# An attention and feed-forward block: one group of value products per kv head, rotated rows and late pages on GpSimd, new rank shifts

## The chip, the cores and the metric

One core of a Trainium2 chip runs the whole program. Time is device time in microseconds (us) from start to end of one execution. The core's engines are TensorE (PE; its weight loads are PEld), VectorE (DVE), ScalarE (ACT), GpSimd (POOL) and SyncE (SP), which here issues most of the DMAs. Each has a queue of its own that runs in program order; between queues there are semaphores.

## What is computed

```python
q = (x @ wq).reshape(4, 512, 32, 32); k, v = (x @ wk), (x @ wv)   # 8 kv heads of 32
q, k = _apply_rope(q, cos, sin), _apply_rope(k, cos, sin)
k, v = jnp.repeat(k, 4, axis=2), jnp.repeat(v, 4, axis=2)
scores = einsum('bqhd,bkhd->bhqk', q, k) / sqrt(32) + causal_mask
out = einsum('bhqk,bkhd->bqhd', softmax(scores), v).reshape(4, 512, 1024) @ wo
x = _layernorm(x + out)
gate_w, up_w, down_w = gate_t * gate_s[:, None], up_t * up_s[:, None], down_t * down_s[:, None]
x = _layernorm(x + (silu(x @ gate_w.T) * (x @ up_w.T)) @ down_w.T)   # 1024 -> 3584 -> 1024
```

x is 4 x 512 x 1024 in float32; gate_t, up_t and down_t are integers from -1 to 1.

## The kernel before

A float32 operand is held as two float16 parts, an upper one (a copy rounded to float16) and a lower one (what is left), and a product of two such operands is three matmuls. Work goes in 128-row tiles: 4 batches of 4 tiles. Attention is done in 16 units of 8 query heads, which is 2 kv heads each, and the code names a kv head of a unit by G. In order:

- **Pages.** Slices of x, wq, wkv and wo arrive by DMA as pages of 128x1024 (`page_load` on SP), ScalarE makes the upper part (`split_hi`, L1241) and VectorE the lower part (`split_lo`, L1384). The first 12 pages (`NFIRST`) have room of their own; the 24 late ones (wq of the units 2 and 3, all of wo, x of the batches 1 to 3) go through two buffers in turn, so a load waits for both parts of the page two before.
- **Projections** (L1070) into two banks by turns. For q and k VectorE forms two products with the rope tables (`rotate`, L1403 and L1405), GpSimd adds them (`rope_add`, L1631), ScalarE writes the upper part twice into rows to be stacked (`nat_hi`, L1257: 128x256 in, read twice, 128x512 out), GpSimd the lower part (`nat_lo`, L1638), and a DMA transposes the rows into q_stack or k_stack (`stack` on SP, L1703). There are 80 such rows: 64 of q, 16 of k. Two buffers (`NNAT`) are used in turn.
- **Row sums.** `score_q` (L1086) makes the scores with queries on the rows, VectorE takes the maximum (`row_max`, L1414 to L1420), ScalarE the sum of the exponentials (`row_sum`, L1280), and maxima and logarithms of the sums become three more rows of q_stack (`max_rows`, by DMA).
- **Products with the values.** `score_k` (L1111) makes the scores with keys on the rows, so that the exponential (`exp`, L1266) gives the final weights in p_tiles. For each kv head the key tiles go from 3 down to 0, with 128, 256, 384 and 512 query columns for each of 4 heads, in 1, 2, 4 and 4 instructions. GpSimd zeroes the upper triangle of the diagonal block (`causal`, L1645). TensorE multiplies with the values (`pv`, L1127) in float32, 4 heads side by side in the array, in groups of `VALUE_TILES` = 2 key tiles: tiles 3 and 2 as one group, which starts when tile 2 is masked, tiles 1 and 0 as another, which starts when tile 0 is masked. Every tile has one buffer in p_tiles. ScalarE and VectorE copy the bank out in two parts (`att_hi`, L1273, `att_lo`, L1457).
- **Output projection** (also L1070), layer norm (`norm_stats` on VectorE, `newton` on GpSimd, L1652 to L1656, `norm` on ScalarE), and seven forms of the result per pair of tiles (`x1_form` on GpSimd, `x1_hi`, `x1_lo`), stored and loaded again transposed as x_forms (L1760).
- **Feed-forward part**, from about 680 us on: seven products instead of eight for gate and up (L1170) and for most of down (L1211), the last ones plain (L1195).

The order in every queue is fixed when the kernel is built. `Plan.put` (L269) gives each piece an engine, a rank in us, an assumed duration, and the pieces that it follows; to the rank the number for its kind in `SHIFTS` (L232) is added. `Plan.close` (L279) then walks through time and gives every engine, whenever it is free, the able piece with the smallest rank. Pairs of kinds in `AT_ONCE` (L246) may follow each other on one engine with no assumed delay. The result is only an order; the semaphores decide when a piece runs.

## Time and profile before

| | us |
|---|---|
| median of 3 runs (1777.97 to 1781.43) | 1781.22 |
| the profiled execution | 1779.99 |
| its span, first to last instruction | 1778.2 |
| busy: TensorE | 1711.6 |
| busy: VectorE | 1208.3 |
| busy: ScalarE | 967.4 |
| busy: GpSimd | 409.1 |

The profile is one execution. Busy time counts an instruction from start to end; a matmul's end is modelled, and matmuls overlap, so a busy TensorE may still lose a little between them. Lines are those of the kernel's source. A wait is put down to the engine that released it last. The granted clock of TensorE is given as a share of full speed; 1.00 is 2.4 GHz.

### The profile page before, as it was taken

Reading aid. Unit: us, or ns where it says so; the run is one execution under the profiler, and the core shown is the slowest. Engines: PE = TensorE matmul, PEld = TensorE weight load, DVE = VectorE, ACT = ScalarE, POOL = GpSimd, SP = SyncE. Lnnn points to the kernel's source line nnn. Section 1 sums busy time; section 2 is a strip of 40 time slices with the busy share of each in tenths; the row PEclk is TensorE's granted clock in tenths of the full one; section 3 lists DMA queues with packets and bytes.
Section 4 is the critical chain, followed back from the end, with each engine's and each line's share of the span. In section 5 each row is a group of like instructions: output and inputs, shape, how many; then the busy total and the mean of one; then the engine's idle time right before and its main releaser. Section 6 shows DMA issues by size and latency. Waiting matters only on the chain.

```text
span 1778.2 us, 26642 instructions
## 1 busy us (share of the span) xinstructions
PE 1711.6 (96%) x9456; PEld 824.8 (46%) x9456; DVE 1208.3 (68%) x2593; ACT 967.4 (54%) x2201; POOL 409.1 (23%) x782
## 2 busy tenths in 40 slices
PE   7979999999999999999999999999999999999998
PEld 4634555555455434444444444444444444443444
DVE  7776668478667744677877768746667666678456
ACT  6799989789978874472553543531323233231321
POOL 3324445445434442410000002103100000003113
PEclk9999999999999999999999999999999999999999
DMA  8543345335235698582653545658312112133202
GB/s 266 104 141 61 70 114 144 61 96 155 56 67 138 163 222 297 170 300 95 207 173 130 202 159 194 219 146 195 115 60 87 42 65 86 42 110 106 96 13 83
DMA packets 228004, 233.44 MB, mean 131 GB/s; under 512 B 183200, under 2 KB 183840, under 8 KB 227872
## 3 DMA queue, kind: packets, MB, share of 16 engines
q1 hardware_dynamic: 224704, 222.86, 42.9%
q10 hardware_dynamic: 3168, 8.88, 1.3%
q8 instruction: 75, 1.23, 0.3%
q14 instruction: 57, 0.47, 0.1%
HBM read 122.78 MB, written 72.88 MB: 110 GB/s over the span
## 4 chain that ended last, share of the span: by engine, by line
PE 71%; DVE 9%; DMA 8%; ACT 8%; issue 2%; POOL 1%; SPq 1%; DVEq 0%; ACTq 0%; POOLq 0%
PE bank L1170 31%; PE bank L1070 13%; PE bank L1211 12%; PE bank L1195 6%; ACT bank L1280 3%; PE bank L1111 3%; PE bank L1127 3%; PE bank L1086 2%; DMA w_page<-gateT 2%; DMA x_forms<-x_forms_spill 1%; ACT p_tiles L1266 1%; DMA w_page<-upT 1%; DMA q_stack<-max_rows 1%; DMA x_forms_spill<-x_parts 1%; DVE acc L1620 1%
## 5 line engine op out<-in xcount | busy, mean ns | idle before, releaser
L1170 PE MATMUL bank<-x_forms,weight_forms 128*128 128x512 f16 x3136 | 705.0, 379 | 7.8 <-DVE up_blocks L1566 4.1
L1170 PEld LDWEIGHTS bank<-x_forms,weight_forms 128*128 128x128 f16 x3136 | 305.4, 98 | 382.4 <-issue 9.9
L1280 ACT ACTIVATE bank<-bank,row_max 128x512 f32<-128x512 f32 (+3 forms) x512 | 265.3, 541 | 21.1 <-DVE row_max L1420 13.5
L1211 PE MATMUL bank<-down_forms 128*128 128x512 f16 x1120 | 267.4, 379 | 7.3 <-DVE acc L1601 7.3
L1420 DVE CUSTOM_DVE_ANT_0 bank<-bank,cmask 128x256 f32<-128x256 f32 (+2 forms) x384 | 206.6, 580 | 85.4 <-PE bank L1086 84.3
L1266 ACT ACTIVATE p_tiles<-bank 128x512 f32<-128x512 f32 (+1 forms) x352 | 194.7, 597 | 44.2 <-PE bank L1111 42.8
L1070 PE MATMUL bank<-wq_parts,xT_parts 128*128 128x256 f16 x1536 | 204.3, 276 | 8.6 <-DVE wq_parts L1380 8.0
L1601 DVE TENSOR_TENSOR acc<-bank,acc 128x512 f32<-128x512 f32 x248 | 167.2, 686 | 59.3 <-PE bank L1211 58.0
L1662 POOL TENSOR_TENSOR acc<-acc,down_forms 128x1024 f32<-128x1024 f32 x16 | 40.2, 2527 | 695.6 <-DVE acc L1601 695.6
L1645 POOL TENSOR_SCALAR_AFFINE_SELECT p_tiles<-p_tiles 128x128 f32<-128x128 f32 (+2 forms) x352 | 123.7, 358 | 231.2 <-ACT p_tiles L1266 227.9
L1211 PEld LDWEIGHTS bank<-down_forms 128*128 128x128 f16 x1120 | 108.7, 98 | 142.2 <-DVE acc L1601 13.1
L1070 PEld LDWEIGHTS bank<-wq_parts,xT_parts 128*128 128x128 f16 x1536 | 150.6, 99 | 49.8 <-DVE wq_parts L1380 8.0
L1070 PE MATMUL bank<-wo_parts,att_parts 128*128 128x512 f16 x672 | 163.6, 380 | 3.3 <-DMA att_parts<-att_spill 3.2
L1086 PE MATMUL bank<-k_stack,q_stack 96*128 96x512 f16 (+3 forms) x512 | 118.8, 302 | 16.9 <-ACT bank L1280 9.4
L1111 PE MATMUL bank<-q_stack,k_stack 99*128 99x512 f16 (+1 forms) x352 | 117.6, 365 | 12.5 <-DMA q_stack<-max_rows 6.0
L1360 ACT ACTIVATE down_forms<-gate_blocks 128x512 f16<-128x512 f32 x92 | 57.6, 626 | 131.6 <-DVE gate_blocks L1576 120.9
L1280 ACT ACTIVATION_READ_ACCUMULATOR bank<-bank,row_max 128x1 f32 x512 | 126.3, 247 | 0.0
L1566 DVE TENSOR_TENSOR up_blocks<-bank,up_blocks 128x512 f32<-128x512 f32 x84 | 57.8, 689 | 96.8 <-ACT up_blocks L1337 67.3
L1348 ACT ACTIVATE gate_blocks<-gate_blocks,gate_scale 128x512 f32<-128x512 f32 x84 | 60.3, 719 | 106.4 <-DVE gate_blocks L1566 106.4
L1195 PE MATMUL bank<-down_forms 128*128 128x512 f16 (+1 forms) x528 | 110.9, 373 | 0.0
L1070 PEld LDWEIGHTS bank<-wo_parts,att_parts 128*128 128x128 f16 x672 | 64.8, 98 | 75.2 <-issue 6.6
L1337 ACT ACTIVATE up_blocks<-bank 128x512 f32<-128x512 f32 x84 | 49.9, 594 | 88.9 <-PE bank L1170 88.7
(124 smaller groups left out, 1990.8 us busy)
## 6 DMA issues: line engine op xcount, KB each, us to landing
weight_forms_spill<-weight_forms SPq DMA_DIRECT2D x28, 896.0 KB, 5.6
weight_forms<-weight_forms_spill SPq DMA_DIRECT2D x28, 896.0 KB, 4.6
...
```

The costliest lines, as they stand in the source:

```text
L1070: t = nc.tensor.matmul(dst, left[:, a, k, rows], right[:, c, k, cols], start=k == 0 and m == 0, stop=last)
L1086: t = nc.tensor.matmul(to[:, h, :], qT[0:STK, u % QS, h0 + h, i * P:n], kT[0:STK, b % 2, kv_of(u, h0 + h), 0:n], start=h == 0, stop=h == R ...
L1111: nc.tensor.matmul(to, kT[0:STKM, b % 2, (u % UNITS) * UG + G, lo:lo + P], qT[0:STKM, u % QS, heads, lo:S], start=True, stop=True).then_in ...
L1170: t = nc.tensor.matmul(strassen[bank_set(use)][to][:, :], w_form[:, use % 4, A_FORMS[a_form], k * P:(k + 1) * P], xF[:, :, B_FORMS[b_form] ...
L1195: t = nc.tensor.matmul(to[:, 0:cols.stop - cols.start], hid_p[place_of(r)][:, k, a, i // 2 * P:(i // 2 + 1) * P], wd_p[place_of(r)][:, c, ...
L1211: t = nc.tensor.matmul(to[:, :], hid_f[r % NF % 3][:, HID_FORMS.index(a_form), a, pair * P:(pair + 1) * P], wd_f[r % NF % 3][:, DOWN_B[b_f ...
L1266: nc.scalar.activation(p32[j][:, h0:h0 + heads, :], bank[5 + m % 2][:, 0:heads * n].rearrange("p (h c) -> p h c", c=n), ACT.Exp, scale=SCO ...
L1280: nc.scalar.activation(scores, scores, ACT.Exp, scale=SCORE_DOWN if mask_added(i) else -1.0, bias=mx[:, u % 2, i, h:h + 1], accum_out=row_ ...
L1348: nc.scalar.activation(gate_t[:, k, :], src, ACT.Silu, scale=sg[:, 2 * (n % NF) + r:2 * (n % NF) + r + 1]).then_inc(s_silu, 1)
L1420: t = nc.vector.tensor_tensor_reduce(scores[:, h, :], scores[:, h, :], cmask[:, S - n:S], -SCORE_DOWN, -MASKED, ALU.add, ALU.min, mx[:, u ...
L1601: nc.vector.tensor_tensor(dst, got[:, :], dst, ALU.add).then_inc(s_acc, 1)
L1645: nc.gpsimd.affine_select(out=block, in_=block, compare_op=ALU.is_ge, fill=0.0, base=0, pattern=[[0, KEY_HEADS[j]], [1, P]], channel_multi ...
```

## The change

Three things are changed together.

1. `VALUE_TILES` goes from 2 to 4: the products with the values of all four key tiles of a kv head are one group. It is issued when the last tile (0) is masked. Inside the group the order 3, 2, 1, 0 stays, and so do the counts that the next head's exponentials wait for.
2. `nat_hi` moves from ScalarE to GpSimd, as a tensor_copy with the same input and output, so that rope_add, nat_hi and nat_lo of a row all run on GpSimd. `split_hi` of the 24 late pages moves from ScalarE to GpSimd too, as a tensor_scalar multiplication, and counts on a semaphore of its own. A late page_load waits for the lower part alone. Two small DMAs that ScalarE issued ahead of a late page now go with the last first page.
3. All of `SHIFTS` is new, which changes the order in every queue, and two pairs are added to `AT_ONCE`.

The diff, its core:

```diff
@@ -90,7 +90,7 @@
 
 KEY_HEADS = (1, 1, 2, 4)
 
-VALUE_TILES = 2
+VALUE_TILES = 4
 KEY_USES = [(G, j, h) for G in range(UG) for j in reversed(range(NT)) for h in range(0, REP, KEY_HEADS[j])]
 NKEY = len(KEY_USES)
 
...
@@ -230,21 +230,21 @@
 
 
 SHIFTS = {
-    PE: {"down": 20, "max_tr": 17, "product": 45, "proj_out": -9, "proj_q": 126, "pv": 12, "score_k": 5, "score_q": 13},
-    SC: {"exp": 328, "hid_hi": -4, "ln_exp": 32, "nat_hi": 381, "norm": 21, "row_sum": 156, "silu": 43, "split_hi": 54,
-         "v_copy": -17, "w_cast": 233, "x1_hi": 8, "x1_store": 1},
-    VE: {"acc": 3, "add_x1": -55, "att_lo": 195, "bound": 21, "d_form": 40, "ds_scale": 6, "hid_form": 9, "hid_lo": 37,
-         "hidden": 55, "ln_seed": -2, "ln_step": 43, "max_copy": 218, "max_parts": 9, "norm_stats": 76, "residual": -4,
-         "rotate": -64, "row_max": 53, "split_lo": 31, "sum": 14, "w_form": 60, "x1_lo": 18},
-    PO: {"nat_lo": 7, "newton": -12, "rope_add": -45, "scale_row": 11, "x1_form": -2},
-    SY: {"att_load": -3, "att_store": 58, "bound_load": -34, "bound_store": -16, "d_in": -20, "d_store": 64, "ds_load": -20,
-         "last_x1": -2, "max_rows": -14, "out_store": 11, "page_load": -4, "row_load": -4, "stack": 11, "w_in": -30, "w_load": 19,
-         "w_store": -24, "xF_load": 130, "xF_store": 3},
+    PE: {"down": -1, "max_tr": 21, "product": 8, "proj_out": -4, "proj_q": 13, "pv": 23, "score_k": 9, "score_q": 17},
+    SC: {"att_hi": -8, "copy": -9, "exp": 29, "hid_hi": -1, "ln_exp": 3, "norm": -10, "row_sum": 35, "silu": 4, "v_copy": -118,
+         "w_cast": 64, "x1_hi": -171, "x1_store": 5},
+    VE: {"acc": -72, "add_x1": -45, "att_lo": 136, "bound": 6, "d_form": 3, "hid_form": -7, "hid_lo": 11, "hidden": 42,
+         "ln_seed": 33, "ln_step": 21, "max_copy": -9, "max_parts": 4, "norm_stats": 17, "residual": 122, "rotate": -2,
+         "row_max": 37, "split_lo": 93, "sum": -73, "w_form": 92, "x1_lo": -6},
+    PO: {"causal": 49, "nat_hi": -4, "nat_lo": -15, "newton": 56, "rope_add": 29, "scale_row": -9, "split_hi": 17, "x1_form": 59},
+    SY: {"att_load": 1, "att_store": -1, "bound_load": -29, "bound_store": -12, "d_in": 4, "d_store": 201, "ds_load": -33,
+         "last_x1": -45, "max_rows": -2, "out_store": 59, "page_load": -18, "stack": 4, "w_in": -18, "w_load": 10, "w_store": -16,
+         "xF_load": 72, "xF_store": -33},
 }
 
 
 AT_ONCE = {("sum", "hidden"), ("hidden", "hid_form"), ("hid_form", "hid_form"), ("ln_step", "max_parts"), ("d_form", "d_form"), 
-           ("residual", "norm_stats"), ("acc", "norm_stats"), ("x1_form", "x1_form"), ("ln_seed", "ln_step"), ("norm", "x1_store")}
+           ("residual", "norm_stats"), ("acc", "norm_stats"), ("x1_form", "x1_form"), ("ln_seed", "ln_step"), ("norm", "x1_store"), ("rope_add", "nat_hi"), ("nat_hi", "nat_lo")}
 
 
 class Waits:
...
@@ -357,7 +357,7 @@
         last = [loads[n - 1]] if n else []
         put(SY, at, .4, "page_load", what, b, j, moves=2 * FIRST_MOVES if n == 0 else FIRST_MOVES if n < NFIRST else PAGE_MOVES,
             after=[("split_lo", *loads[before])] if before >= 0 else [])
-        put(SC, at, .95, "split_hi", what, b, j, after=[("page_load", what, b, j)] + [("split_hi", *w) for w in last] + (
+        put(SC if n < NFIRST else PO, at, .95 if n < NFIRST else 1.4, "split_hi", what, b, j, after=[("page_load", what, b, j)] + [("split_hi", *w) for w in last] + (
             [("proj", "q", UNITS * b - 1, j, KD - 1)] if what == "x" and b else []))
         put(VE, at, 1.14, "split_lo", what, b, j, after=[("split_hi", what, b, j)] + [("split_lo", *w) for w in last])
 
...
@@ -417,7 +417,7 @@
         put(VE, -195.0 + 2 * t if one[0] == "q" and w == 0 and t < 2 else end, .72, "rotate", *one, after=[made] + ([("rotate", *one_back)] if r else []) + (
             [("nat_lo", *two_back), ("rope_add", *two_back)] if r > 1 else []))
         put(PO, end + 1, .68, "rope_add", *one, after=[("rotate", *one)])
-        put(SC, end + 2, .53, "nat_hi", *one, after=[("rope_add", *one)] + ([("nat_hi", *one_back)] if r else []) + ([("stack", *two_back)] if r > 1 else []))
+        put(PO, end + 2, .72, "nat_hi", *one, after=[("rope_add", *one)] + ([("nat_hi", *one_back)] if r else []) + ([("stack", *two_back)] if r > 1 else []))
         put(PO, end + 3, .68, "nat_lo", *one, after=[("nat_hi", *one)] + ([("nat_lo", *one_back)] if r else []))
         old = w - QS if one[0] == "q" else UNITS * (w - 1) - 1
         put(SY, end + 4, 1.25, "stack", *one, moves=TURN_MOVES, after=[("nat_lo", *one)] + ([("stack", *one_back)] if r else []) + (
...
@@ -1223,15 +1223,11 @@
                         e.dma_start(idH[:, :], identH).then_inc(s_const, 16)
                         e.dma_start(idB[:, :], identB).then_inc(s_const, 16)
                         e.dma_start(cmask[:, :], causal).then_inc(s_const, 16)
-                    elif n == NFIRST + 2:
+                    elif n == NFIRST - 1:
                         e.dma_start(sg[:, :], gate_s).then_inc(s_scale, 16)
                         e.dma_start(su[:, :], up_s).then_inc(s_scale, 16)
                     src, arrived, times = page_of(n)
                     on.wait_ge(arrived, 16 * times)
-                    if which[0] == "wo":
-                        on.wait_ge(s_lo, NFIRST)
-                    if which[0] == "x" and which[1]:
-                        on.wait_ge(s_proj, proj_n["q", which[1] * UNITS - 1, which[2]] + 1)
                     up = X_UP if which[0] == "x" else W_UP
                     hi, whole = parts_of(*which)[0], as_parts(which[0], src)
                     if n < HALVED:
...
@@ -1246,16 +1242,6 @@
                     on.wait_ge(s_pv, (b - 1) * UNITS * UG * NT)
                     nc.scalar.activation(v32[:, b % 2, t, :], bank[n % 2][:, nk:2 * nk], ACT.Copy,
                                          scale=PROJ_DOWN).then_inc(s_v, 1)
-                elif kind == "nat_hi":
-                    r = rot_n[which]
-                    on.wait_ge(s_add, r + 1)
-                    on.wait_ge(s_set, 1)
-                    on.wait_ge(s_stack[r % NNAT], 16 * (r // NNAT))
-                    rows = nat[:, r % NNAT, :, 0:STK].rearrange("p h (f c) -> p h f c", f=3)
-                    fields = slice(0, 3, 2) if which[0] == "k" else slice(0, 2)
-                    ta = ropeA[:, r % NNAT, :].rearrange("p (h c) -> p h c", h=UH)
-                    nc.scalar.activation(rows[:, :, fields, :], ta.unsqueeze(2).broadcast_to([P, UH, 2, HD]),
-                                         ACT.Copy).then_inc(s_nhi, 1)
                 elif kind == "exp":
                     u, G, j, h0 = which
                     m, q, heads, n = key_n(*which), u * UG + G, KEY_HEADS[j], S - j * P
...
@@ -1380,7 +1366,10 @@
                         nc.vector.scalar_tensor_tensor(lo[:, 0:mid], whole[:, 0:mid], up, hi[:, 0:mid],
                                                        ALU.mult, ALU.subtract).then_inc(s_half_lo, 1)
                         hi, lo, whole = hi[:, mid:], lo[:, mid:], whole[:, mid:]
-                    on.wait_ge(s_hi, n + 1)
+                    if n < NFIRST:
+                        on.wait_ge(s_hi, n + 1)
+                    else:
+                        on.wait_ge(s_hi_late, n - NFIRST + 1)
                     nc.vector.scalar_tensor_tensor(lo, whole, up, hi, ALU.mult, ALU.subtract).then_inc(s_lo, 1)
                 elif kind == "rotate":
                     what, w, t = which
...
@@ -1629,6 +1618,25 @@
                     on.wait_ge(s_proj_taken, taken["rotate", what, w, t])
                     to = ropeA[:, r % NNAT, :]
                     nc.gpsimd.tensor_tensor(to, to, ropeB[:, r % 2, :], ALU.add).then_inc(s_add, 1)
+                elif kind == "nat_hi":
+                    r = rot_n[which]
+                    on.wait_ge(s_add, r + 1)
+                    on.wait_ge(s_set, 1)
+                    on.wait_ge(s_stack[r % NNAT], 16 * (r // NNAT))
+                    rows = nat[:, r % NNAT, :, 0:STK].rearrange("p h (f c) -> p h f c", f=3)
+                    fields = slice(0, 3, 2) if which[0] == "k" else slice(0, 2)
+                    ta = ropeA[:, r % NNAT, :].rearrange("p (h c) -> p h c", h=UH)
+                    nc.gpsimd.tensor_copy(rows[:, :, fields, :], ta.unsqueeze(2).broadcast_to([P, UH, 2, HD])).then_inc(s_nhi, 1)
+                elif kind == "split_hi":
+                    n = split_n[which]
+                    src, arrived, times = page_of(n)
+                    on.wait_ge(arrived, 16 * times)
+                    if which[0] == "wo":
+                        on.wait_ge(s_lo, NFIRST)
+                    if which[0] == "x":
+                        on.wait_ge(s_proj, proj_n["q", which[1] * UNITS - 1, which[2]] + 1)
+                    nc.gpsimd.tensor_scalar(parts_of(*which)[0], as_parts(which[0], src), X_UP if which[0] == "x" else W_UP, None,
+                                            ALU.mult).then_inc(s_hi_late, 1)
                 elif kind == "nat_lo":
                     r = rot_n[which]
                     on.wait_ge(s_add, r + 1)
...
@@ -1687,7 +1695,6 @@
                     n = split_n[which]
                     dst, arrived, times = page_of(n)
                     if n >= NFIRST + 2:
-                        on.wait_ge(s_hi, n - 1)
                         on.wait_ge(s_lo, n - 1)
                     e.dma_start(as_parts(which[0], dst), source_of(*which)).then_inc(arrived, 16)
                 elif kind == "stack":
```

## Rows read from the trace of the kernel before

**Rows 1.** The page, busy time by engine: us, share of the span, instructions.

```profile
PE 1711.6 (96%) x9456; PEld 824.8 (46%) x9456; DVE 1208.3 (68%) x2593; ACT 967.4 (54%) x2201; POOL 409.1 (23%) x782
```

**Rows 2.** Stretches: busy us of PE, PEld, DVE, ACT, POOL; clock, DMA share, GB/s.

```profile
46.00:92.00 46.00, 41.68 (x342) 31.26 (x341) 36.70 (x119) 35.46 (x110) 17.65 (x27) 0.96 0.51 103
92.00:138.00 46.00, 35.45 (x235) 16.48 (x233) 34.76 (x103) 44.37 (x131) 13.88 (x34) 0.93 0.50 140
138.00:598.00 460.00, 450.52 (x3276) 243.12 (x3275) 313.89 (x971) 403.75 (x1185) 212.88 (x455) 1.00 0.40 96
598.00:690.00 92.00, 82.19 (x468) 32.73 (x465) 50.73 (x128) 63.23 (x151) 39.04 (x90) 0.98 0.96 232
690.00:1196.00 506.00, 496.99 (x2290) 222.46 (x2290) 361.10 (x608) 230.16 (x328) 51.14 (x47) 1.00 0.55 188
...
1250.00:1778.00 528.00, 515.47 (x2398) 233.69 (x2396) 341.90 (x545) 152.47 (x236) 40.65 (x66) 1.00 0.21 75
```

**Rows 3.** Waits in 46 to 138: who <- for whom, total us, times, longest.

```profile
PE bank L1086 <- ACT bank L1280: 5.8, 6, 2.6
...
PE bank L1111 <- ACT p_tiles L1266: 2.4, 4, 0.9
```

**Rows 4.** Waits in 138 to 598, same columns.

```profile
PEld bank L1111 <- ACT p_tiles L1266: 21.8, 57, 0.9
...
POOL stack_rows L1638 <- ACT stack_rows L1257: 16.1, 31, 2.8
PEld bank L1086 <- ACT bank L1280: 15.6, 46, 0.8
...
PEld bank L1127 <- POOL p_tiles L1645: 4.8, 14, 0.4
```

**Rows 5.** Waits of TensorE in 598 to 690.

```profile
PE bank L1070 <- DMA att_parts<-att_spill: 2.3, 2, 2.1
```

**Rows 6.** Timeline: start us, us, engine, line, instructions, [idle before <- releaser].

```profile
332.86 0.86 PE L1127 MATMUL bank<-p_tiles,v 128*32 128x128 f32 x16
...
333.65 0.39 PE L1111 MATMUL bank<-q_stack,k_stack 99*128 99x512 f16 x1
...
340.47 0.29 POOL L1645 TENSOR_SCALAR_AFFINE_SELECT p_tiles<-p_tiles 128x128 f32<-128x128 f32 x1 [0.19 <-ACT p_tiles L1266]
...
340.71 1.18 ACT L1266 ACTIVATE p_tiles<-bank 128x512 f32<-128x512 f32 x2
...
341.18 1.71 PE L1127 MATMUL bank<-p_tiles,v 128*32 128x384 f32 x16
...
342.82 0.55 PE L1111 MATMUL bank<-q_stack,k_stack 99*128 99x512 f16 x2
343.02 0.60 ACT L1273 ACTIVATE att_made<-bank 128x512 f16<-128x512 f32 x1 [0.61 <-PE bank L1127]
```

**Rows 7.** Groups of ScalarE in 92 to 138: count | busy us, mean ns | idle before.

```profile
L1241 ACT ACTIVATE wo_parts<-page 128x1024 f16<-128x1024 f32 x4 | 4.3, 1075 | 0.5 <-DMA page<-wo 0.5
L1257 ACT ACTIVATE stack_rows<-rope_cos 128x512 f16<-128x512 f32 x4 | 2.9, 734 | 0.0
L1241 ACT ACTIVATE xT_parts<-page 128x1024 f16<-128x1024 f32 x2 | 2.1, 1064 | 0.1
```

**Rows 8.** Groups of ScalarE in 138 to 598.

```profile
L1257 ACT ACTIVATE stack_rows<-rope_cos 128x512 f16<-128x512 f32 x58 | 38.9, 696 | 2.3 <-POOL rope_cos L1631 1.7 <-DMA q_stack<-stack_rows 0.5
...
L1241 ACT ACTIVATE xT_parts<-page 128x1024 f16<-128x1024 f32 x8 | 8.5, 1064 | 0.0
```

**Rows 9.** Groups of GpSimd by form, whole run.

```profile
L1662 POOL TENSOR_TENSOR acc<-acc,down_forms 128x1024 f32<-128x1024 f32 x16 | 40.2, 2527 | 695.6 <-DVE acc L1601 695.6
...
L1645 POOL TENSOR_SCALAR_AFFINE_SELECT p_tiles<-p_tiles 128x512 f32<-128x512 f32 x32 | 20.4, 639 | 31.2 <-ACT p_tiles L1266 31.2
...
L1672 POOL TENSOR_TENSOR x_difference<-row 128x512 f32<-128x512 f32 x7 | 8.9, 1274 | 8.1 <-ACT row L1299 8.1
```

**Rows 10.** One line's instructions: count, duration ns min/median/max, first and last start.

```profile
L1384 DVE SCALAR_TENSOR_TENSOR wq_parts<-page,wq_parts x4: 1224/1456/1749, 24.9 to 34.4; 128x1024 f16<-128x1024 f32 x4
```

8 lines of the change are left out of this document (4 added, 4 removed).

## Prediction

> **What bounds the kernel now.** Three runs gave a median of 1781.2 us. The profiled execution took 1780.0, of which 1778.2 is its span, so the sum below starts from 1780.0 and the median lies 1.2 above it. The first view to read is the page: TensorE is busy for 1711.6 us, 96% of the span, while ScalarE, VectorE and GpSimd have 54, 68 and 23% [rows 1]. So the kernel is bound by TensorE where its queue is full, and only two things can make it shorter: a matmul stream that needs less time, or idle TensorE time that is filled. The second view, the stretches, says where that idle time is [rows 2]. The reader takes TensorE's busy time from the length of each: 4.3 us of 46 are idle in 46 to 92, 10.6 in 92 to 138, 9.5 in the 460 us from 138 to 598, 9.8 in 598 to 690, 9.0 in 690 to 1196, and 12.5 in 1250 to 1778. In all that is 56 us (3.1%), which is about the ceiling of any better order; of the whole span 1778.2 - 1711.6 = 66.6 are idle, and the rest of that lies before 46.
>
> Which engine ends those waits differs by stretch. In 92 to 138 ScalarE is busy 44.4 of 46 us and TensorE's granted clock falls to 0.93. There, and in the stretch ahead of it, TensorE's waits name ScalarE: 5.8 us for row sums and 2.4 for exponentials, 8.2 of the 14.9 that are idle [rows 3]. In 138 to 598 ScalarE is at 403.8 of 460 (88%), and TensorE's weight loads wait for it 21.8 + 15.6 us [rows 4], most of which a running matmul covers, since TensorE is idle for 9.5 in all. In 598 to 690 the DMA share is 0.96, and a DMA, of att_parts, heads TensorE's waits [rows 2, 5]. After 690 the change moves no work between engines; ScalarE is busy less than half of that time.
>
> **One group of products instead of two.** A group of 16 records for the tiles 3 and 2 streams 128 + 256 = 384 columns; from its start to the next matmul's it takes 333.65 - 332.86 = 0.79 us. The group for the tiles 1 and 0 streams 512 + 384 = 896 columns in 342.82 - 341.18 = 1.64 [rows 6]. Taken as a fixed part plus a part per column, 0.85 us for 512 more columns is 1.66 ns a column, and 0.79 - 384 x 0.00166 leaves 0.15 us fixed. The 32 pairs of groups (16 units, 2 kv heads each) become 32 groups: 32 x 0.15 = 4.9 us of TensorE's time go. If the fixed part is an effect of the pipeline that next to no issue hides, all of it is gained; if it is drain that other waits swallow, nothing is. I take **-4.9**, bounds 0 and -5.
>
> **What the group now waits for.** It starts after the causal mask on the last exponentials (tile 0), and the exponentials of the next head may write tile 3 only when this group's product with tile 3 is done. Rows 6 show the present overlap. The last causal mask of one head begins at 340.47; ScalarE has the next head's first exponentials on at 340.71, before the second group starts at 341.18. With one group, started in the same place, tile 3 is free at 341.18 + 0.15 + 128 x 0.00166 = 341.54, and with the 0.2 us from an end to the engine it releases (the group ends at 342.82, ScalarE's copy of it starts at 343.02) ScalarE has it at about 341.75: the exponentials pause **1.0 us more per head**, 32 us in all. Queued behind them on ScalarE, in the order fixed when the kernel is built, stand row sums and later exponentials; behind the group on TensorE stand projections. Cover: for each kv head there are 16 row sums (one for each of 4 tiles of 4 heads), which can be placed in the pause, and TensorE has the projections' matmuls. If the cover is gone, each of the 32 costs up to 1.0 us. It is thinnest for the last kv heads, when all row sums are done. I take **+2**, bounds 0 and +32.
>
> **ScalarE is relieved.** 80 copies of rotated rows (0.70 us each) and 24 conversions of late pages (1.06) leave it [rows 8], 56 + 25 = 81 us. Where it is worth something: in 92 to 138 there are 4 copies and 6 conversions, 2.9 + 4.3 + 2.1 = 9.3 us [rows 7] of a full ScalarE, against 10.6 us of idle TensorE and a clock of 0.93 (46 x 0.07 = 3.2 us lost while busy or idle). I take 6 of the 9.3, since a wait on VectorE's maxima or a page's DMA may come close behind, and 1 for the clock: **-7**, bounds -12 and 0. In 138 to 598, 58 copies and 8 conversions, 38.9 + 8.5 = 47.4 us [rows 8], leave an engine that would then be at (403.8 - 47.4) / 460 = 77%; of the 9.5 idle us there I take **-2**, bounds -9 and 0.
>
> **GpSimd takes it.** The trace has neither operation there. The nearest row with one input is the mask of 128x512, 0.64 us (the same rows); with two inputs, 128x512 takes 1.27 and 128x1024 takes 2.53 [rows 9]. So a copy of 128x512 costs 0.64 to 1.27 and a conversion of 128x1024 1.28 to 2.53; both have one input, and I take the lower ends with a little more, 0.7 and 1.4: 80 x 0.7 + 24 x 1.4 = 90 us, at the upper ends 162. GpSimd is busy for 17.7 + 13.9 + 212.9 + 39.0 = 283 of the 644 us from 46 to 690 [rows 2], 44%; it becomes 58 to 69%. In the rotation's chain it saves two changes of engine (GpSimd stands 16.1 us waiting for ScalarE's copies in 138 to 598, rows 4), and the projections run a unit and more ahead of the scores that use them, so the chain itself costs nothing; without that lead, it is 80 x 0.2 us at most. What counts is what waits behind these on GpSimd: the causal masks, and behind the last of each head the products. 24 conversions of 1.4 us and 80 copies of 0.7 cover 90 of 640 us, so 14% of the 32 masks that release a group meet one, for half its length: 32 x 0.14 x 0.5 = 2.2 us. A page is also converted 0.4 us later and reloaded later; the loads lose a wait on the upper part that the wait on the lower part implies. I take **+1**, bounds 0 and +6. SP's queue keeps its instructions; it waits for other producers only.
>
> One thing could make these operations dearer. The same lower-part instruction on VectorE takes from 1.224 to 1.749 us [rows 10], so something in this kernel holds VectorE up. With each of the 24 late lower parts put off by 1.749 - 1.224 = 0.525, 12.6 us come onto VectorE, which is busy for 385 of the 552 us from 46 to 598 [rows 2]; that costs nothing in the sum, and at worst, if GpSimd's masks are held up in turn, the bound of +6. The Trainium skill (SBUF — State Buffer, section on the two physically separate sides) names a cause that speaks against the move: the port pair of these two engines is an exclusive lock, taken for a whole instruction by a GpSimd operation or by a VectorE operation with two SBUF inputs. The spread in rows 10 agrees with it; by that rule the sum would be the same or go to +6 here.
>
> **The new shifts** reorder every queue. q projections fall from 126 to 13, so they no longer only fill gaps; ScalarE's exponentials go from 328 to 29. No row prices that. In 598 to 690 there are 9.8 idle us to win; a reordering of x_forms loads and projections can win or lose 5. After 690 there are 21.5, of which the chain behind the last matmul stays. I take -1 for 598 to 690, **0** after, and keep 6 each way.
>
> **Sum.** -4.9 + 2 - 7 - 2 + 1 - 1 = -11.9; 1780.0 - 11.9 = 1768.1, and 1.2 for the median: **1769 us**, 0.7% faster. Its own range is 1762 to 1776.
>
> **The rivals.** *The relief does not arrive.* Another wait (VectorE's maxima, page DMAs) ends last in 92 to 138, and TensorE gets the 4.9 us less 3 of new waits: 1781.2 - 1.9 = 1779. For it: only in 92 to 138 is ScalarE full; in the 46 us before it stands idle for 10.5 itself, and the work of TensorE there does not shrink. Chance 0.15. *Slower: the ring of one group.* Exponentials, mask, products and next exponentials become one chain per head, 1.0 us longer, on engines whose order is fixed. The place is 138 to 690, where TensorE is 97% busy. It decides from the point where 14 of the 32 pauses reach TensorE, for the gains are 4.9 + 7 + 2 + 1 = 14.9 and GpSimd takes 1 of them. If three in four do, and the masks are 3 us late in all, it is 24 + 3 - 14.9 = +12: 1781.2 + 12 = 1793. Against it: now only 4.8 us of weight loads in 460 wait for a mask [rows 4]. Chance 0.24. *Slower by order alone:* the shifts cost 5 at 598 to 690 and 6 in the feed-forward part, nothing is gained but the groups: 1781.2 - 4.9 + 11 = 1787. Chance 0.06. *More is won:* the first stretches and the x_forms stage both close (-12 there, -5, -5 after 690, -5 for groups, +3): 1757. Chance 0.13. That the moved work shows no shorter ScalarE at all is excluded by the diff.
>
> **How the numbers follow.** The forecast has the remaining 0.42. Measurements of this kernel can tell about 0.2%, 3.6 us, from no change. Faster by more: 0.42 + 0.13 + 0.05 of the first rival = 0.60; within: 0.12, the rest of the first rival and what of the slower cases ends near; slower: 0.28. The range reaches from 1756 to 1790: it holds the forecast, the first rival, the order case, most of the larger gain and the nearer half of the ring.
>
> **What would show it.** Right: in the changed profile ScalarE falls by some 80 us and GpSimd rises by some 90; the products of a head stand as one run of 32 records of about 2.3 us; the idle time of TensorE near 92 to 138 is under 5 us with the clock near 1.00. Wrong: in 138 to 598 the weight loads' waits for exponentials, row sums and masks, now 21.8 + 15.6 + 4.8 = 42.2 us [rows 4], double; page conversions of over 2 us on GpSimd; or new idle time after 690, which would be the shifts'.

## The result and the profile after

The changed kernel is slower: 1798.3 us median of 4 runs (1794.09 to 1803.54) against 1781.3 of the kernel before (1777.97 to 1782.24, 4 runs). The ratio is 1.0085, with a 95% interval of 1.0059 to 1.0112. The forecast was 1769, and the time lies outside its range of 1756 to 1790. The profiled execution took 1794.09, and its span is 1792.4, 14.2 longer than before. Four executions of the runs further down were over 10% above their kernel's others, and the medians leave them out.

First the page of the changed kernel, busy time by engine (us, share of the span, instructions):

```profile
PE 1714.0 (96%) x9456; PEld 829.1 (46%) x9456; DVE 1220.8 (68%) x2593; ACT 906.0 (51%) x2097; POOL 530.8 (30%) x886
```

Against [rows 1], ScalarE lost 61 us (80 were expected) and GpSimd gained 122 (90 were expected). The group rows of the copies and conversions that left ScalarE add up to 53.2 + 25.5 = 78.7 us; the records of its instructions overlap in part, and the busy time counts an overlap once, so it fell by less. TensorE's idle time, span less busy time, went from 66.6 to 78.4 us, and its busy time rose by 2.4, though the products with the values went from 84.0 to 78.8. The 11.8 us of idle time and the 2.4 of busy time make up the 14.2.

The stretches of the changed kernel say where (busy us of PE, PEld, DVE, ACT, POOL; clock, DMA share, GB/s):

```profile
20.00:46.00 26.00, 21.44 (x123) 11.86 (x122) 16.72 (x20) 3.35 (x13) 25.62 (x16) 0.93 0.56 135
...
46.00:92.00 46.00, 41.17 (x316) 30.04 (x315) 38.44 (x133) 32.08 (x117) 35.96 (x44) 0.96 0.60 114
92.00:138.00 46.00, 38.25 (x295) 20.39 (x294) 33.73 (x88) 33.85 (x104) 45.85 (x51) 0.96 0.44 116
138.00:598.00 460.00, 433.35 (x3080) 233.69 (x3078) 316.89 (x953) 352.97 (x1086) 259.54 (x493) 0.98 0.41 97
598.00:690.00 92.00, 83.65 (x543) 36.84 (x542) 57.18 (x152) 69.62 (x179) 42.82 (x99) 1.00 0.84 194
690.00:1196.00 506.00, 500.46 (x2330) 224.01 (x2329) 359.78 (x613) 235.98 (x335) 55.08 (x65) 1.00 0.56 193
```

Three things stand out beside [rows 2]. From 20 to 46 GpSimd is busy for 25.6 of 26 us, and from 92 to 138 for 45.85 of 46: it is now the full engine there, while ScalarE, which was full, is down to 33.9. From 138 to 598 TensorE is idle for 26.7 us instead of 9.5, with a clock of 0.98 instead of 1.00; how much of that belongs to the moved pages is a question for the experiments. After 690 nothing is lost: 5.5 idle us instead of 9.0 up to 1196. The weight loads of the feed-forward part tell the same (count: ns min/median/max, first and last start), before and after:

```profile
L1170 PEld LDWEIGHTS bank<-x_forms,weight_forms x3136: 95/98/99, 680.6 to 1714.3; 128*128 128x128 f16 x196
```

```profile
L1170 PEld LDWEIGHTS bank<-x_forms,weight_forms x3136: 95/98/99, 699.4 to 1728.4; 128*128 128x128 f16 x196
```

The first starts at 680.6 before and at 699.4 after. So 18.8 us are lost ahead of it and 4.6 of them won back behind it.

What GpSimd is busy with, by group and form (count | busy us, mean ns | idle before, releaser):

```profile
L1646 POOL TENSOR_TENSOR stack_rows<-rope_cos,stack_rows 128x256 f16<-128x256 f32 x80 | 60.9, 761 | 2.8
L1629 POOL CAST stack_rows<-rope_cos 128x512 f16<-128x512 f32 x80 | 52.6, 657 | 3.3 <-DMA q_stack<-stack_rows 1.3
L1638 POOL TENSOR_SCALAR xT_parts<-page 128x1024 f16<-128x1024 f32 x12 | 33.4, 2784 | 0.1
L1638 POOL TENSOR_SCALAR wo_parts<-page 128x1024 f16<-128x1024 f32 x8 | 24.4, 3049 | 0.9 <-DMA page<-wo 0.9
L1638 POOL TENSOR_SCALAR wq_parts<-page 128x1024 f16<-128x1024 f32 x4 | 13.0, 3260 | 0.0
```

The 80 copies cost 0.657 us each, as expected (0.7). The 24 page conversions cost 2.8 to 3.3 each in the mean of their groups, 70.8 us in all, where 1.4 each and 33.6 in all were assumed; the shortest of them takes 2.76, so even the upper bound, 2.53 from [rows 9], is below every one.

How that reaches TensorE is seen in the timeline of the changed kernel (start us, us, engine, line; GpSimd's stream around 130 and the products that wait for it):

```profile
124.19 2.77 POOL L1638 TENSOR_SCALAR xT_parts<-page 128x1024 f16<-128x1024 f32 x1
126.93 1.52 POOL L1653 TENSOR_SCALAR_AFFINE_SELECT p_tiles<-p_tiles 128x128 f32<-128x128 f32 x2
...
128.43 2.77 POOL L1638 TENSOR_SCALAR wo_parts<-page 128x1024 f16<-128x1024 f32 x1
131.15 2.26 POOL L1653 TENSOR_SCALAR_AFFINE_SELECT p_tiles<-p_tiles 128x128 f32<-128x128 f32 x5
...
133.38 2.77 POOL L1638 TENSOR_SCALAR wo_parts<-page 128x1024 f16<-128x1024 f32 x1
...
133.47 2.36 PE L1127 MATMUL bank<-p_tiles,v 128*32 128x128 f32 x32 [1.94 <-POOL p_tiles L1653]
...
136.82 3.74 POOL L1638 TENSOR_SCALAR wo_parts<-page 128x1024 f16<-128x1024 f32 x1
```

Between 124 and 141 four conversions stand on GpSimd, with causal masks and one `rope_add` (at 136.12) between them, without a gap. Five masks follow at once behind the second conversion, so they had piled up, and TensorE stands idle for 1.94 us until the last of them. TensorE's waits over the whole changed kernel sum this up (who <- for whom, total us, times, longest):

```profile
PE bank L1127 <- POOL p_tiles L1653: 10.0, 5, 3.3
PE bank L1111 <- DMA q_stack<-max_rows: 9.4, 8, 2.7
PE bank L1111 <- ACT p_tiles L1252: 9.3, 17, 1.2
...
PE bank L1070 <- DVE rope_sin L1394: 5.6, 2, 4.6
```

The first line has no counterpart before: 10.0 us of products waiting for masks. The last, 1.4 before, is a second way on which the conversions reach TensorE, and 4.6 of its 5.6 us are one wait. It stands in the timeline of the same kernel around 30:

```profile
27.33 3.74 POOL L1638 TENSOR_SCALAR wq_parts<-page 128x1024 f16<-128x1024 f32 x1
...
31.17 1.54 DVE L1373 SCALAR_TENSOR_TENSOR wq_parts<-page,wq_parts 128x1024 f16<-128x1024 f32 x1 [2.74 <-POOL wq_parts L1638]
32.63 0.41 DVE L1392 TENSOR_TENSOR rope_cos<-bank,rope_tab 128x256 f32<-128x256 f32 x1
32.97 0.41 DVE L1394 TENSOR_TENSOR rope_sin<-bank,rope_tab 128x256 f32<-128x256 f32 x1
33.43 7.04 PE L1070 MATMUL bank<-wkv_parts,xT_parts 128*128 128x512 f16 x24 [4.56 <-DVE rope_sin L1394]
```

VectorE waits 2.74 us for GpSimd's upper part of a page, makes the lower part, and only then comes to `rotate`, which stands behind it in its queue and empties the bank that the projection needs. Over the run VectorE waits 6.3, 7.3 and 9.4 us for GpSimd's parts of wq, wo and x. In TensorE's waits the exponentials are further up from 5.7 to 9.3 and the `max_rows` DMA from 6.0 to 9.4. These two are as long when the pages are back on ScalarE (9.8 and 11.2 in e5 below), so they come with the other parts, while the waits for masks and for `rotate` fall to 0.3 and 1.8 there.

### The profile page after: what moved, and what is told of

Read it like the earlier page. It is cut to its first block, busy times and chain, and to the rows that moved or that the text cites. A ratio compares the mean times of both kernels' runs of the same rounds, so it can differ in the third digit from the quotient of the medians.

```text
span 1792.4 us, 26514 instructions
## 1 busy us (share of the span) xinstructions
PE 1714.0 (96%) x9456; PEld 829.1 (46%) x9456; DVE 1220.8 (68%) x2593; ACT 906.0 (51%) x2097; POOL 530.8 (30%) x886
## 4 chain that ended last, share of the span: by engine, by line
PE 71%; DVE 8%; DMA 6%; POOL 6%; ACT 4%; issue 4%; SPq 1%; DVEq 0%; ACTq 0%; POOLq 0%
PE bank L1170 34%; PE bank L1211 12%; PE bank L1070 11%; PE bank L1195 6%; PE bank L1111 2%; PE bank L1086 2%; PE bank L1127 2%; DMA q_stack<-max_rows 2%; ACT bank L1266 1%; DMA x_forms<-x_forms_spill 1%; DMA x_forms_spill<-x_parts 1%; ACT p_tiles L1252 1%; POOL p_tiles L1653 1%; POOL xT_parts L1638 1%; DVE bank L1409 1%
## 5 line engine op out<-in xcount | busy, mean ns | idle before, releaser
L1170 PEld LDWEIGHTS bank<-x_forms,weight_forms 128*128 128x128 f16 x3136 | 305.4, 98 | 381.5 <-issue 12.8
L1266 ACT ACTIVATE bank<-bank,row_max 128x512 f32<-128x512 f32 (+3 forms) x512 | 265.9, 529 | 70.8 <-DVE row_max L1409 62.7
L1070 PE MATMUL bank<-wq_parts,xT_parts 128*128 128x256 f16 x1536 | 214.5, 275 | 8.1 <-DVE wq_parts L1366 8.1
L1653 POOL TENSOR_SCALAR_AFFINE_SELECT p_tiles<-p_tiles 128x128 f32<-128x128 f32 (+2 forms) x352 | 127.8, 375 | 184.4 <-ACT p_tiles L1252 182.5
L1070 PE MATMUL bank<-wo_parts,att_parts 128*128 128x512 f16 x672 | 167.4, 385 | 2.9 <-DMA att_parts<-att_spill 2.7
L1111 PE MATMUL bank<-q_stack,k_stack 99*128 99x512 f16 (+1 forms) x352 | 121.7, 368 | 19.3 <-DMA q_stack<-max_rows 9.4
L1086 PE MATMUL bank<-k_stack,q_stack 96*128 96x512 f16 (+3 forms) x512 | 123.1, 304 | 9.0 <-ACT bank L1266 3.5
L1266 ACT ACTIVATION_READ_ACCUMULATOR bank<-bank,row_max 128x1 f32 x512 | 119.4, 233 | 0.0
L1070 PE MATMUL bank<-wkv_parts,xT_parts 128*128 128x512 f16 x384 | 98.0, 384 | 5.6 <-DVE rope_sin L1394 5.6
L1660 POOL TENSOR_SCALAR rstd<-rstd 128x1 f32<-128x1 f32 x93 | 34.8, 375 | 227.9 <-DVE rstd L1470 221.7
```

The costliest lines, as they stand in the source:

```text
L1070: t = nc.tensor.matmul(dst, left[:, a, k, rows], right[:, c, k, cols], start=k == 0 and m == 0, stop=last)
L1086: t = nc.tensor.matmul(to[:, h, :], qT[0:STK, u % QS, h0 + h, i * P:n], kT[0:STK, b % 2, kv_of(u, h0 + h), 0:n], start=h == 0, stop=h == R ...
L1111: nc.tensor.matmul(to, kT[0:STKM, b % 2, (u % UNITS) * UG + G, lo:lo + P], qT[0:STKM, u % QS, heads, lo:S], start=True, stop=True).then_in ...
L1170: t = nc.tensor.matmul(strassen[bank_set(use)][to][:, :], w_form[:, use % 4, A_FORMS[a_form], k * P:(k + 1) * P], xF[:, :, B_FORMS[b_form] ...
L1266: nc.scalar.activation(scores, scores, ACT.Exp, scale=SCORE_DOWN if mask_added(i) else -1.0, bias=mx[:, u % 2, i, h:h + 1], accum_out=row_ ...
L1653: nc.gpsimd.affine_select(out=block, in_=block, compare_op=ALU.is_ge, fill=0.0, base=0, pattern=[[0, KEY_HEADS[j]], [1, P]], channel_multi ...
```

## The experiments

"Order kept" means that every queue keeps the order of the kernel it is made from; a moved piece goes to its new queue at the time at which the planner had placed it, and groups are merged or split in place. Every difference below is one of medians, in us. Three theories stand against each other in what was expected: 'pages' (the conversions of late pages are dear on GpSimd and hold up what waits there), 'ring' (exponentials, mask, one group of products and the next exponentials form a longer chain) and 'order' (the new shifts give a worse order). The runs were made in four groups (e1 to e4, e5 to e8, e9 to e12, e13 to e16), each with runs of the kernel before beside it, whose medians were 1781.0, 1781.6, 1781.2 and 1781.7. A difference to the kernel before is taken within the group, as is the ratio; one to the changed kernel or between groups carries up to 1 us of that spread.

### The suspect: the page conversions

**Late pages back on ScalarE** (e5_pages_back), changed kernel, order kept:

```diff
     plan.close()
+    plan.move("split_hi", PO, SC, lambda w: w not in FIRST)
```

> The changed kernel, its order kept; only the upper parts of the 24 late pages go back to ScalarE, inserted in its queue at the time that the planner had for them on GpSimd. 'Pages' (two runs now speak for it: 1811 with them alone, 1772 with a cheap copy in their place): 1770 to 1782, GpSimd 70 us less busy, ScalarE 25 us more. 'Ring' or 'order': 1790 or more.

Measured: 1774.6, ratio to before 0.9957 (0.9943 to 0.9970). With this one part undone, 23.7 us go and the kernel beats both. Its stretch from 92 to 138 (columns as above):

```profile
92.00:138.00 46.00, 42.12 (x313) 22.32 (x314) 36.59 (x115) 44.62 (x140) 23.32 (x47) 1.00 0.66 159
```

GpSimd is half idle, ScalarE is full again, and yet TensorE is busy for 3.9 us more than in the changed kernel, at a clock of 1.00. The time expected was 1770 to 1782.

**The same conversions, cheaper, in the same place** (e4_cheap_pages), changed kernel, order kept:

```diff
-                    nc.gpsimd.tensor_scalar(parts_of(*which)[0], as_parts(which[0], src), X_UP if which[0] == "x" else W_UP, None,
-                                            ALU.mult).then_inc(s_hi_late, 1)
+                    nc.gpsimd.tensor_copy(parts_of(*which)[0], as_parts(which[0], src)).then_inc(s_hi_late, 1)
```

> The changed kernel, its order kept to the instruction; only the conversion of a late page on GpSimd is a plain copy to float16 in place of the multiplication (this leaves out the factor 64 or 256 on the upper part, so the values are not the reference's). By the 0.66 us of the 128x512 copy it should take 1.2 to 1.4 us instead of 2.8 to 3.3. 'Pages': 37 us less of GpSimd, so 1776 to 1786. 'Ring' or 'order': 1793 to 1800.

Measured: 1772.1, ratio 0.9937 (0.9916 to 0.9958), faster than all three theories had it. The result of this kernel is wrong by the missing factor, so it serves for its time alone; e5, whose result is right, comes out near it. GpSimd's groups:

```profile
L1647 POOL CAST xT_parts<-page 128x1024 f16<-128x1024 f32 x12 | 13.7, 1145 | 0.8 <-PE bank L1079 0.8
L1647 POOL CAST wo_parts<-page 128x1024 f16<-128x1024 f32 x8 | 9.3, 1161 | 4.1 <-DMA page<-wo 4.1
L1647 POOL CAST wq_parts<-page 128x1024 f16<-128x1024 f32 x4 | 6.1, 1534 | 0.0
```

and the stretch from 92 to 138:

```profile
92.00:138.00 46.00, 43.96 (x329) 22.45 (x327) 40.62 (x124) 41.78 (x141) 33.20 (x58) 1.00 0.70 163
```

Shape, types, tiles, place and order are the same; the instruction is a copy instead of a multiplication. The 24 take 29.1 us instead of 70.8, 1.21 each in the mean instead of 2.95, and the end comes 26.2 us earlier. So it is the duration of these 24 instructions that makes the changed kernel slow, and not that they stand on GpSimd: at 1.21 us each they do no worse there than on ScalarE (2.5 us better, with intervals that overlap).

Where the time goes is told by TensorE's idle and busy time in the profiled executions, split at 138 us and at the first weight load of the feed-forward part (at 680.6, 699.4, 676.4 and 675.7):

| us of TensorE, granted clock | before | changed | e5 | e4 |
|---|---|---|---|---|
| idle, 0 to 138 | 25.6 | 25.3 | 16.3 | 12.8 |
| clock, 0 to 138 | 0.96 | 0.96 | 1.00 | 1.00 |
| matmul records up to 138 | 780 | 797 | 888 | 922 |
| idle, from 138 to that load | 18.7 | 35.0 | 29.9 | 28.3 |
| clock, from 138 to that load | 1.00 | 0.98 | 0.99 | 0.98 |
| busy, up to that load | 636.4 | 639.1 | 630.3 | 634.5 |
| idle, behind it | 22.4 | 18.2 | 20.7 | 20.0 |

Against e5, the changed kernel has 9.0 us more idle time ahead of 138, 5.1 more between 138 and that load, 8.9 more busy time for the same 4480 matmuls, and 2.6 less idle time behind. Against the kernel before the picture misleads: all its additional idle time lies behind 138, but 11.2 of those 16.3 us are in e5 too, which is faster than the kernel before. They come with the other parts of the change, not with the pages.

**The pages alone in the kernel before** (e3_pages_alone), order kept, the move of e5 the other way round:

> The kernel before, its order kept; only the upper parts of the 24 late pages go to GpSimd, inserted in its queue at their planned time. 'Pages': 24 x 2.8 us come onto GpSimd, most of them before 140 us, so 1790 to 1800, with the lost time before 140. 'Ring' and 'order': within 4 of 1781.

Measured: 1810.9, ratio 1.0164 (1.0147 to 1.0180), so +30 without any other part. That is 11 above the upper end of what 'pages' had, and the loss is not all before 140 either: TensorE's idle time rises by 6.0 us up to 138 and by 14.5 from there to the feed-forward part. The conversions take 2.98 to 3.26 us in the mean of their groups. The stretch shows that the clock pays too, 0.81 where [rows 2] have 0.93:

```profile
92.00:138.00 46.00, 34.70 (x209) 16.44 (x207) 33.77 (x92) 31.59 (x101) 38.17 (x34) 0.81 0.41 134
```

**Which pages.** In the changed kernel, order kept, the 12 of wq and wo go back to ScalarE (e13_weights_back; they start from 22.9 to 136.8), or the 12 of x (e14_x_back; 89.1 to 453.6):

```diff
+    plan.move("split_hi", PO, SC, lambda w: w not in FIRST and w[0] != "x")   # e13; == "x" in e14
```

> The changed kernel, its order kept; the 12 late pages of wq and wo have their upper parts on ScalarE again, the 12 pages of x stay on GpSimd. If the loss is the crowd before 140 us (GpSimd full, TensorE short of weights): 1775 to 1783, most of the 24 us back. If it is masks held up by x pages: 1788 to 1797.

> The changed kernel, its order kept; the 12 late pages of x have their upper parts on ScalarE again, the 12 of wq and wo stay on GpSimd. By the crowd before 140 us: 1788 to 1797. By masks held up in the steady part: 1775 to 1783.

Measured: 1782.3 (1.0000, 0.9987 to 1.0014) and 1787.1 (1.0033, 1.0019 to 1.0046), that is 16.0 and 11.2 less than changed. They add up to 27.1, about the 23.7 of all 24. So it is no single place: 1.3 us of the end per page of the weights, 0.9 per page of x. Four of the 12 pages of x start before 138 as well, so the two runs don't part the early crowd from the later masks; e13 lies at the upper end of the range for the crowd, e14 0.9 below it.

**Telling the planner the price** (e8_pages_true_cost): changed kernel, the assumed duration of a late conversion 2.8 instead of 1.4, order made anew.

> The changed kernel, the conversions still on GpSimd, but the planner is given 2.8 us for one instead of 1.4, so only the order changes. If the loss is work that GpSimd has no room for: 1792 to 1800, as the changed kernel. If it is only that the order was made for a wrong price: 1780 or less.

Measured: 1789.1, ratio 1.0037 (1.0023 to 1.0051). Better by 9.2, but not by 24, and between the two ranges. It is one order; that no order could hide 70 us of conversions is not shown.

**Pages planned and run on ScalarE** (e7_pages_planned_back), order made anew:

> The changed kernel with the late pages' upper parts on ScalarE (0.95 us in the planner, shift 0), and the whole order made anew from that; rows on GpSimd, one group and the new shifts stay. 'Pages': 1768 to 1782, below before. 'Ring' or 'order': 1790 or more.

Measured: 1779.8, ratio 0.9993 (0.9977 to 1.0008), 5.2 above the same parts with the order kept (e5). What a new order costs by itself is measured further down.

### The rival: the ring of one group

**One group alone in the kernel before** (e1_group_alone). Order kept, the group issued in the place of its second half; where the third exponential's scores of the next head stood ahead of that, the group goes in front of them: they use the bank of the first exponentials again, and those wait for tile 3.

```diff
     plan.close()
+    plan.regroup()          # drops the pieces ("pv", (u, G, 2)) from TensorE's queue
+    VALUE_TILES = 4
```

> The kernel before, its order kept in every queue; only the two groups of value products of a kv head become one, at the place of the second (moved ahead of the next head's third score product where it stood behind it). Theory 'pages' (the late page conversions cost GpSimd 2.8 to 3.3 us each instead of the 1.4 that was assumed, and masks, rows and page loads queue behind them): the group alone costs nothing or gains its fixed part, 1776 to 1782. Theory 'ring' (exponentials, mask, products and the next head's exponentials form one longer chain): 1793 or more, with TensorE waiting for p_tiles. Theory 'order' (the new shifts give a worse order): as 'pages', within 5 of before.

Measured: 1804.1, ratio 1.0135 (1.0112 to 1.0158), +23. With 'pages' as the only cost it would have come to 1776 to 1782, so one group has a cost of its own here. TensorE's waits for row sums (L1112 is `score_q` in this kernel) and for exponentials (L1137, `score_k`), to be read beside 9.4 and 5.7 us for the same two in the kernel before:

```profile
PE bank L1112 <- ACT bank L1306: 18.5, 27, 3.1
PE bank L1137 <- ACT p_tiles L1292: 14.1, 31, 1.0
```

and the weight loads' waits in 138 to 598, 21.8 and 15.6 in [rows 4]:

```profile
PEld bank L1137 <- ACT p_tiles L1292: 43.4, 86, 1.5
PEld bank L1112 <- ACT bank L1306: 22.4, 50, 1.4
```

ScalarE's own waits name the mechanism: the exponentials wait for the products with the values (L1153 here) of the head before.

```profile
ACT p_tiles L1292 <- PE bank L1153: 22.8, 19, 2.7
```

Neither the kernel before nor the changed kernel nor e5 has a wait of the exponentials for these products. So the ring is real in the old order, and in the new order the exponentials don't wait for the group.

**One group or two, pages on ScalarE, new order kept** (e15_two_groups_pages_back, to be compared with e5):

> The changed kernel, its order kept, late pages back on ScalarE and two groups per kv head instead of one. Against 1774.6 with one group. If one group is worth its fixed part in an order made for it: 1777 to 1784, as two groups cost 8 us with the pages on GpSimd. If the pages' crowd made that difference: 1770 to 1776.

Measured: 1780.2, ratio 0.9995 (0.9982 to 1.0008). One group is thus 5.6 us better than two in this order. The group of the products in e15 (1024 records; busy us, mean ns; idle before):

```profile
L1150 PE MATMUL bank<-p_tiles,v 128*32 128x128 f32 (+3 forms) x1024 | 82.9, 441 | 0.6 <-POOL p_tiles L1667 0.5
```

and in e5:

```profile
L1137 PE MATMUL bank<-p_tiles,v 128*32 128x128 f32 (+3 forms) x1024 | 75.6, 435 | 0.3 <-POOL p_tiles L1654 0.3
```

The products take 82.9 us of TensorE in two groups per head and 75.6 in one, and they wait for next to nothing in either.

**Two groups in the changed kernel** (e6_two_groups), order kept, pages still on GpSimd:

> The changed kernel, its order kept; only the one group of value products of a kv head becomes two again, the first (tiles 3 and 2) put 0.8 us behind the planned time of tile 2's last mask. 'Ring' as a cost that the new order did not remove: 1785 to 1793. If the new order had made room for the longer chain, the second group's fixed part is all that comes back: 1798 to 1804.

Measured: 1806.4, ratio 1.0132 (1.0112 to 1.0153), 8.1 worse than changed. So the ring is not what the changed kernel loses by. (By the expectation, 1798 to 1804 was the reading for an order with room for the longer chain; the time lies just above it.)

**One group planned** (e10_group_planned): the kernel before with `VALUE_TILES = 4` given to the planner too, old shifts, order made anew.

> The kernel before with one group per kv head and the order made anew, old shifts, rows and pages on ScalarE. The group alone in the old order cost 23 us (1804). If any order that knows of the longer chain hides it: 1776 to 1786. If it takes the new shifts or the lighter ScalarE: 1790 to 1805.

Measured: 1818.4, ratio 1.0210 (1.0182 to 1.0237). Both ranges are missed. This order is 14 worse than the old one kept (e1), so telling the planner of the longer chain did not help here.

### The rows

**The copies alone in the kernel before** (e2_rows_alone), order kept, with `plan.move("nat_hi", SC, PO, lambda w: True)`:

> The kernel before, its order kept; only the 80 copies of rotated rows go to GpSimd, inserted in its queue at their planned time. In the changed kernel they take 0.66 us each there. All three theories: between 1774 and 1783. A gain of 5 or more would say that ScalarE's relief is worth something by itself; over 1785, that the copies are a part of the loss.

Measured: 1785.6, ratio 1.0031 (1.0015 to 1.0047), +4.6, above what all three theories had (1774 to 1783): in the old order the move of the copies is a part of the loss.

**Rows and pages both back in the changed kernel** (e12_rows_back_too), order kept, to be compared with e5, in which the rows stay on GpSimd:

> The changed kernel, its order kept, with late pages and rotated rows both back on ScalarE at their planned times; the group of four and the new order stay. Against the run with pages back alone (1774.6) this puts 53 us on ScalarE again. If the rows' move relieves a path: 1779 to 1792. If it is worth nothing, as in the old order (1785.6 with it, 1781 without): 1771 to 1777.

Measured: 1783.7, ratio 1.0015 (0.9999 to 1.0031). In the new order the rows are worth 9.1 us on GpSimd; in the old one they cost 4.6.

### The order

**New shifts alone** (e9_shifts_alone), all parts as before:

> The kernel before with only the new shifts (groups of two tiles, rows and pages on ScalarE, where these two kinds have shift 0 now), order made anew. If a new order by itself brings what the changed kernel has once its pages are cheap (1772 to 1775): 1770 to 1777. If the shifts are only good for the other parts: 1778 to 1795.

Measured: 1802.0, ratio 1.0116 (1.0089 to 1.0142), +21, above both ranges.

**All parts, old shifts** (e11_old_shifts):

> The changed kernel with the shifts of before (the three kinds on GpSimd that the old table does not name get shift 0), order made anew. 'Pages' costs 24 us in the new order; if the old shifts are no worse for it: 1793 to 1803. If the new shifts make room for pages and group: 1805 to 1825.

Measured: 1827.9, ratio 1.0261 (1.0235 to 1.0287), +46.8, or 29.6 above the changed kernel.

**What any other order costs** (e16_shifts_jittered): the kernel before, each shift 2 us up or down.

```diff
-    PE: {"down": 20, "max_tr": 17, "product": 45, "proj_out": -9, "proj_q": 126, "pv": 12, "score_k": 5, "score_q": 13},
+    PE: {"down": 18, "max_tr": 15, "product": 47, "proj_out": -11, "proj_q": 128, "pv": 14, "score_k": 7, "score_q": 15},
```

> The kernel before with every shift moved up or down by 2, order made anew, nothing else. It measures what an order that is not the chosen one costs. If orders near the chosen one are alike: 1778 to 1785. If any new order costs: 1788 or more, and the replanned runs (the new shifts alone, 1802; the group planned, 1818) show little of their own part.

Measured: 1792.2, ratio 1.0062 (1.0041 to 1.0083). This one change of all shifts by 2 costs 10.5 us. A difference of 10 between two orders made anew therefore says little on the part that was changed, which is why the parts above are judged with the order kept. A kept order has a bias too: it was made for the parts of its kernel, so undoing one of them there can cost something by the misfit alone. For the pages that makes the finding stronger, since undoing them gained 23.7 us; for the group (5.6) and the rows (9.1) a share of the figure may be misfit, and no run parts the two.

## Why the prediction was wrong

**The step that failed is "GpSimd takes it".** It put the conversions and copies at +1 us, bounds 0 and +6 (its own rule gave 2.2, and it took 1 without a reason). The pages alone were worth +23.7 in the changed kernel (against e5), and +30 in the old order (e3). Two things in that step were wrong.

*The price.* It took the mask of 128x512, 0.64 us, as nearest row "with one input" and came to 1.4 us per page, with 2.53 of the two-input sum as the upper end. Measured is 2.76 at the least. The number of inputs was the wrong measure of nearness: the copy with one input (CAST) goes as the mask does, 0.66 us for 512 elements and 1.15 for 1024, while the multiplication by a constant (TENSOR_SCALAR), with one input as well, costs more than the sum of two inputs. The copy of rows and the conversion of pages are different instructions, and one price was argued for both. "The trace has neither operation there" holds for the shape only. The instruction form of the conversion did stand on GpSimd, in `newton`, at one element per partition, so that it gave no price per element:

```profile
L1654 POOL TENSOR_SCALAR rstd<-rstd 128x1 f32<-128x1 f32 x93 | 36.9, 397 | 9.5
```

So no row bounded its price at 1024 elements, and 2.53 was no upper end for it. The prediction named the sign, "page conversions of over 2 us on GpSimd", but its bounds didn't reach it.

*How it reaches TensorE.* "14% of the 32 masks meet one, for half its length" spreads the moved work evenly over 640 us and counts only what stands behind it on GpSimd. The trace has 16 of the 24 conversions between 22.9 and 140.6, eight of them in 92 to 138, and there GpSimd has next to no idle time left: 25.6 of 26 us from 20 to 46, 45.85 of 46 from 92 to 138. Where the engine has no idle time left, nothing absorbs the added time, and all that is queued behind it comes later. And the step left VectorE out, where the lower part waits for the upper one with `rotate` queued behind it (the timeline around 30 above). Between e4 and the changed kernel GpSimd's conversions differ by 41.7 us and the end by 26.2, 0.63 of them; the prediction's rule gave 2.2 us for 90 us of moved work, 0.02. The average of 44% for 46 to 690 hid this. At the measured prices its rule would have given 32 x (70.8 / 640 x 1.5 + 52.6 / 640 x 0.33) = 6 us, a quarter of the 23.7, so price and path both failed.

**One group: -4.9.** Right in size. In the changed trace the group of 32 records takes 326.25 - 323.96 = 2.29 us, against 0.79 + 1.64 = 2.43 of [rows 6]:

```profile
323.96 2.36 PE L1127 MATMUL bank<-p_tiles,v 128*32 128x128 f32 x32
326.25 0.40 PE L1086 MATMUL bank<-k_stack,q_stack 96*128 96x128 f16 x4
```

0.14 us by 32 heads is 4.5, and e15 against e5 is 5.6. The bounds of 0 and -5 are crossed by that, within the spread of such a difference.

**The ring: +2, bounds 0 and +32.** In the old order it measured 23.1, or 27.6 when the gain of 4.5 is added back, 0.86 per head where 1.0 was the price. In the new order the group gains about all of its 4.9, so the ring costs next to nothing there. The price per head and both bounds stood. What decides between them is the order, which the prediction couldn't cost. Its test, the weight loads' waits for exponentials, row sums and masks in 138 to 598, gives 32.6 + 15.3 + 4.5 = 52.4 after against 42.2 before, not double:

```profile
PEld bank L1111 <- ACT p_tiles L1252: 32.6, 94, 1.5
...
PEld bank L1086 <- ACT bank L1266: 15.3, 35, 0.8
...
PEld bank L1127 <- POOL p_tiles L1653: 4.5, 2, 2.4
```

The forecast's main rival on the slow side was thus the wrong mechanism, though its time, 1793, is near the measured one.

**ScalarE's relief: -7 and -2.** ScalarE is busy for 61 us less, not 80. In the changed kernel the gain is covered up. With cheap pages (e4) it can be seen ahead of 138: from 92 to 138 TensorE idles for 2.0 us instead of 10.6, the clock is 1.00, and so "under 5 with the clock near 1.00" holds. Behind 138 it did not come: from there to the feed-forward part TensorE idles for 28.3 us in e4 and 29.9 in e5, against 18.7 before, where -2 was taken. In the new order the rows' move gives 9.1 (e12 against e5), and that of the pages, at 1.21 us each on GpSimd, 2.5 more at best; in the old order the rows' move costs 4.6. So the sum of 9 is met in the new order only, and by another split than the one forecast, which is in part luck.

**The shifts: -1, and 0 after 690.** Behind the first weight load of the feed-forward part 4.6 us are won where 0 was taken, within the 6 each way. As a part by itself the term had no meaning: the new shifts alone cost 21, and without them the other parts cost 46.8. New shifts and moved work are one thing. With pages cheap or back, all other parts together come to 1772.1 and 1774.6, inside the forecast's own range of 1762 to 1776. So the sum without its failed term was good to some 6 us. That is luck in part: two of its terms (ring and shifts) held only together, and the relief came in another place.

**The port between VectorE and GpSimd.** The prediction bounded it within +6. The trace of the changed kernel shows instructions of both engines that take longer where they overlap, once on each side:

```profile
118.69 1.98 POOL L1646 TENSOR_TENSOR stack_rows<-rope_cos,stack_rows 128x256 f16<-128x256 f32 x1
...
118.92 1.20 DVE L1373 SCALAR_TENSOR_TENSOR wo_parts<-page,wo_parts 128x1024 f16<-128x1024 f32 x1
...
136.12 0.72 POOL L1620 TENSOR_TENSOR rope_cos<-rope_cos,rope_sin 128x256 f32<-128x256 f32 x1
136.26 1.67 DVE L1373 SCALAR_TENSOR_TENSOR wo_parts<-page,wo_parts 128x1024 f16<-128x1024 f32 x1 [1.15 <-POOL wo_parts L1638]
...
136.82 3.74 POOL L1638 TENSOR_SCALAR wo_parts<-page 128x1024 f16<-128x1024 f32 x1
```

`nat_lo`, 0.67 us in the median, takes 1.98 around a VectorE lower part of 1.20; a conversion takes 3.74 instead of 2.77 beside a lower part that itself takes 1.67 instead of 1.22, behind the start of a `rope_add`. The Trainium skill (SBUF — State Buffer, section on the two physically separate sides) says that the two engines' shared port pair is locked for a whole instruction; these rows agree with it, since each excess is about as long as the other engine's instruction, or what is left of it. Which engine goes first is not told by the starts: `nat_lo` starts 0.23 us ahead of the lower part and is the one that takes longer. In size it is the smaller matter: 24 conversions at 2.77 would be 66.5 us, and they took 70.8, and the 80 `nat_lo` took 60.9 instead of 54.1 before.

**Left open.** Why the multiplication costs 2.4 times the copy on GpSimd isn't known; whether it is the factor or the instruction's path in general was not separated. A version with the right result and plain copies was not built. Nor is it shown how the pages' cost divides between the masks and VectorE's queue: against e5, TensorE's waits for them rise by 9.7 and 3.8 us, 13.5 together where the idle time rises by 11.5, while the 8.7 of busy time go with a clock of 0.96 instead of 1.00 up to 138 and 0.98 instead of 0.99 behind it, and whose idle time lowered the clock was not taken apart. Why the new order idles more than the old one from 138 on, even without the pages, is open too.
